# A product of zeros ahead of each wait for a landed chunk, in the first message pass of a graph kernel

## What is computed

```python
def rgcn_conv(x, src, dst, etype, W, root, bias):
    seg = dst * R + etype                      # R = 5 relations
    agg = segment_sum(x[src], seg)             # sum of neighbours by relation
    cnt = segment_sum(1, seg)
    agg = where(cnt > 0, agg / max(cnt, 1), 0).reshape(n, R, -1)
    return einsum('nrd,rdk->nk', agg, W) + x @ root + bias
h = relu(rgcn_conv(concat([x, node_emb[node_type]]), ...))     # 256 wide
```

## Time and profile before

| | us |
|---|---|
| median of 3 runs | 6255.49 (6251.28 to 6260.96) |
| the profiled execution, time | 6247.44 |
| its span | 6245.6 |
| TensorE busy | 4417.3 (71%) |
| GpSimd busy | 3267.3 (52%) |
| VectorE busy | 2981.6 (48%) |

### The profile page before, as it was taken

The page is one execution under the profiler, slowest core; times in us unless marked ns, Lnnn a source line. Parts: engine busy times, 40 slices in busy tenths (PEclk is TensorE's granted clock), DMA queues, the critical chain, the costliest instruction groups (busy, mean ns, idle before and its releaser), DMA issues.

```text
span 6245.6 us, 98864 instructions
## 1 busy us (share of the span) xinstructions
PE 4417.3 (71%) x20570; PEld 3106.2 (50%) x20573; DVE 2981.6 (48%) x6741; ACT 1057.7 (17%) x3779; POOL 3267.3 (52%) x3114
## 2 busy tenths in 40 slices
PE   4677676767677777777767777775647777877773
PEld 1223455555565445454544444444645665666652
DVE  5443222222222666667666666666882222222235
ACT  0111111111111111111111111111751111111112
POOL 0000355555554666666666666663325666666650
PEclk7566667777777999999999999997985555555556
DMA  1011223333333122222222222222423333333320
GB/s 67 23 53 53 79 85 93 102 92 102 95 104 106 53 61 72 71 81 81 90 74 61 65 71 77 82 79 74 147 94 85 85 85 85 84 84 85 84 73 11
DMA packets 318265, 492.02 MB, mean 79 GB/s; under 512 B 98090, under 2 KB 221228, under 8 KB 314556
## 3 DMA queue, kind: packets, MB, share of 16 engines
q0 software_dynamic: 108864, 246.74, 14.6%
q1 hardware_dynamic: 209372, 244.94, 11.8%
HBM read 406.11 MB, written 85.29 MB: 79 GB/s over the span
## 4 chain that ended last, share of the span: by engine, by line
issue 24%; POOL 22%; PE 19%; DMA 12%; DVE 9%; another core or an unknown queue 6%; DVEq 3%; ACTq 2%; ACT 2%; POOLq 1%; SPq 0%
POOL msg_r L493 22%; DMA msg_r<-y_tab,idx_r 8%; PE psum L1375 4%; DMA msg_r<-z_tab,idx_r 3%; PE psum L1440 3%; DVE h_t L1132 2%; PE psum L1255 1%; PE psum L1580 1%; DVE hot_r L990 1%; PE psum L1287 1%; PE psum L1267 1%; PE psum L1537 1%; ACT idx_r L578 1%; PE psum L1581 1%
## 5 line engine op out<-in xcount | busy, mean ns | idle before, releaser
L493 POOL DMA_INDIRECT msg_r<-y_tab,idx_r x2160 | 2234.6, 1035 | 2053.2 <-issue 1291.3
L1440 PE MATMUL psum<-shot_r,hotb_r 128*128 128x400 bf16 x5760 | 1313.6, 353 | 573.3 <-DMA msg_r<-y_tab,idx_r 454.8
L493 POOL DMA_INDIRECT msg_r<-z_tab,idx_r x882 | 933.6, 1058 | 511.5 <-issue 323.1
L1440 PEld LDWEIGHTS psum<-shot_r,hotb_r 128*128 128x128 bf16 x5760 | 503.4, 102 | 1009.4 <-DMA msg_r<-y_tab,idx_r 489.2
L1014 DVE TENSOR_SCALAR shot_r<-iota_h,edge_g 128x1600 bf16<-128x1600 f16 x1440 | 906.1, 684 | 0.0
L578 ACT COPY idx_r<-row_i 128x1 int32 x2142 | 409.9, 191 | 2898.6 <-DMA msg_r<-y_tab,idx_r 2643.2
L1580 PE MATMUL psum<-msg_r,shot_r 128*128 128x128 f32 x1764 | 680.2, 488 | 294.3 <-DMA msg_r<-z_tab,idx_r 152.1
L1375 PE MATMUL psum<-hot_r,msg_r 128*128 128x128 f32 x2880 | 634.5, 385 | 319.8 <-DVE hot_r L990 193.9
L1375 PEld LDWEIGHTS psum<-hot_r,msg_r 128*128 128x128 f32 x2880 | 540.9, 277 | 434.3 <-issue 260.9
L1580 PEld LDWEIGHTS psum<-msg_r,shot_r 128*128 128x128 f32 x1764 | 437.2, 308 | 522.8 <-DMA msg_r<-z_tab,idx_r 351.0
L893 DVE TENSOR_TENSOR shot_r<-iota_h,dst_g 128x384 f32<-128x384 f16 x294 | 166.1, 565 | 862.7 <-PE psum L1581 436.7
(11 more groups left out here) (273 smaller groups left out, 3905.3 us busy)
## 6 DMA issues: line engine op xcount, KB each, us to landing
msg_r<-in_attr SPq DMA_DIRECT2D x882, 64.0 KB
h_t<-count_tab SPq DMA_DIRECT2D x25, 1600.0 KB, 6.6
count_tab<-w_s SPq DMA_DIRECT2D x48, 800.0 KB
msg_r<-y_tab,idx_r POOLq DMA_INDIRECT x2160
xn<-heavy_tab SPq DMA_DIRECT2D x76, 320.0 KB
y_tab<-y_s SPq DMA_DIRECT2D x25, 640.0 KB, 2.9
xn<-y_tab SPq DMA_DIRECT2D x25, 640.0 KB
y_tab<-y_s SPq DMA_DIRECT2D x50, 320.0 KB
```

The source lines that it names most:

```text
L493: pool.indirect_dma_start(out=msg_r[:, q, 0:width], out_offset=None, in_=table, in_offset=bass.IndirectOffsetOnAxis(ap=idx_r[:, q:q + 1], ...
L1440: ins = T.matmul(psum[:, 4 + b, 0:CB], hotb_r[:, q, :], shot_r[:, q, b * CB:(b + 1) * CB], start=first, stop=last)
```

## The change

In the first pass TensorE executes one more product ahead of its wait for each chunk's rows: 128 columns of zeros times 512 columns of zeros in bf16, added to the whole bank of the open sums. So that the bank's other 256 columns take part in the open sums, the products that open and close a tile's sums are widened from 256 to 512 columns. What is computed stays the same. Nothing moves on the other engines.

```diff
                 for q in range(U):
                     if q % UH == 0:
                         pe.wait_ge(s_hot[k][q // UH], after)
+                    if k == 0:
+                        T.matmul(psum[:, bass.ds(slot, 1), :].rearrange("p o f -> p (o f)"), zeros_b[:, 0:P], zeros_b[:, :], start=False, stop=False)
                     pe.wait_ge(s_msg[k][q], landed)
...
             def start0(D, slot):
                 pe.wait_ge(s_inv_in, D)
-                clear(acc0(slot, 0, 2))
+                clear(psum[:, bass.ds(slot, 1), :].rearrange("p o f -> p (o f)"))
                 root0(D, lambda m: acc0(slot, m))
...
             def stop0(slot):
-                close(acc0(slot, 0, 2), s_sums[0])
+                close(psum[:, bass.ds(slot, 1), :].rearrange("p o f -> p (o f)"), s_sums[0])
```

## The result

The kernel after took 6277.85 us (median of 13 runs, 6257.29 to 6305.06) beside 6254.11 us for the kernel before (13 runs) on the same chip: a ratio of 1.0038, 95% interval 1.0026 to 1.0049, or 24 us slower. The forecast had the sign, and the time is inside the range, but 76 us were forecast, and 24 us lie outside the likeliest case's own +40 to +120 us. The two profiled executions differ by 17 us (6247.44 and 6264.57).

A forecast was written before the change was run, and what follows sets the result against it. No engine alone was taken to bound the kernel; in the first pass GpSimd's gathers wait for TensorE's chunks, at low clock 0.56 of the time. +91 - 17 + 2 = +76 us gave 6331 us, range 6230 to 6400 us.

The forecast's parts named there:

- likeliest case: Forecast case: low-clock share 0.35 to 0.8 in stretches behind one-hot waits, kernel +40 to +120 us; chance 0.58.
- The price of a product of zeros: A 512-column bf16 product of zeros on TensorE takes 0.22 us at the high clock, 0.44 us at the low.
- 267 zeros on the path, +91 us, less 17 us for the clock.: Three zeros in each of 89 groups with waiting one-hots delay chunks, +91 us; faster chunks give back 17 us.
- The low share of these stretches falls from 0.7 to 0.55: Low-clock share while three chunks run behind a wait for one-hots; the fall gains 17 us on chunks.
- the one-hots start 2.4 us behind the last gather whatever TensorE does: In groups with waiting one-hots, they follow the last gather's issue by 2.4 us, leaving TensorE that much to spare.
- groups that wait for their rows: I take 0: Zeros there run in 0.5 to 0.6 us of idle ahead of each chunk, so cost 0.
- the 2 us for all the other zeros: Each one-hot-waiting group's other three zeros and the widened opening and closing products are hidden ahead of line 1313: 2 us.
- The clock is high nearly everywhere: Rival: 267 zeros cost 59 us, chunks gain 81: -22 us, 6233 us; deciding low share 0.13; chance 0.12.
- The long waits are TensorE's own work at the low clock: Rival: high clock takes 1 us off about 100 VectorE waits, -100 us beside -22: 6135 us; chance 0.06.
- The zeros show everywhere: Rival: low share stays 0.7, other zeros of each tile's first two groups show: +154 us, 6410 us; chance 0.12.

The follow-up runs named there:

- g2: The changed kernel against the kernel before, on another chip of the slow kind: 1.0089, +54 us.
- f3: The changed kernel against the kernel before, on the fast chip: 0.9963, -21 us.
- e4: Kernel before plus widened opening and closing products and three 512-column zero products ahead of each wait for one-hots, none between chunks; slow-kind chip: 0.9969, -18 us.
- f2: Three zero products ahead of each wait for one-hots, none between chunks, against the kernel before on the fast chip: 0.9934, -37 us.
- e8: Eight zero products ahead of a tile's first group's one-hot wait and eight behind its heavy products, against the kernel before, fast chip: 1.0031, +18 us.
- e7: One zero product ahead of each wait for one-hots, two a group, against the kernel before on the fast chip: 0.9951, -28 us.
- e12: One zero product ahead of each wait for one-hots, two a group, against the kernel before on a slow-kind chip: 0.9982, -12 us.
- f4: One zero product directly ahead of each wait for one-hots, against the kernel before on the fast chip: 0.9955.
- f1: One zero product directly behind each wait for one-hots, against the kernel before on the fast chip: 0.9979.
- e11: Kernel before plus two semaphore additions ahead of each chunk's wait for rows, no zeros; slow-kind chip: 1.0039, +22 us.
- e5: Kernel before plus two semaphore additions ahead of each chunk's wait for rows, no zeros; fast chip: 1.0010.
- e10: The changed kernel against the kernel before, on a second slow-kind chip: 1.0082, +48 us.

## Why the prediction was right or wrong

**The price of a product of zeros** holds: 0.22 us high and 0.43 low between the starts of records, as medians of the traces after, g2 and f3 (1426.88 to 1427.10 and 1445.81 to 1446.24 above), where I had 0.22 and 0.44. Three chunks with their zeros take 2.0 us high and 3.8 low (I had 2.2 and 4.1).

**267 zeros on the path, +91 us, less 17 us for the clock.** This is 0.83 us for each of the 89 groups, and where the waits stay as they were it is right. In second groups the stretch from the first of the three chunks, or its zeros, to the end of the third grew by 1.07, 0.88 and 0.91 us on A, C and D, and the groups by 1.04, 0.84 and 0.82; in the first groups of C and D the stretch grew by 0.95 and 0.93. Line 1325 has 87 us of the chain on A and 98 on D (7.8% of 1260). In first groups of A the stretch grew by 0.28 us only, since the low share fell from 0.82 to 0.45. As time lost in the whole pass the term was too large: zeros ahead of the wait (e4, on B) are 42 us better than the change on A, 66 and 72 on C and D, and on F the place is worth 16 to 19 us (f2 against f3).

**"The low share of these stretches falls from 0.7 to 0.55"** holds in size: over all groups but the third it went from 0.73 to 0.58 on A, 0.81 to 0.62 on C and 0.78 to 0.64 on D. It doesn't hold in place. In the first two groups it stays at 0.75 on C and at 0.78 on D, and fell from 0.72 to 0.60 on A; the rest is in fourth and later groups. The chunk products lose 34 us of the chain on A, not 17. The clock of the pass rises more than I had (0.72 to 0.88, against 0.8), much of it in groups that wait for rows: the low share of third groups went to 0.00 and they became longer. The size of e4's gain, 18 us, agrees with the 17 only as a number.

**The step that failed** is that everything but the chunks stays where it is: **"the one-hots start 2.4 us behind the last gather whatever TensorE does",** and with it **"groups that wait for their rows: I take 0"** and the 2 us for all the other zeros. The rows shown for it are of a second group, and I carried it over to all 89. The runs show in its place:

- In first groups the one-hots came earlier after the change: 8.1 us behind the first gather where they had come 9.0 behind it on A (8.4 for 8.9 on C, 8.6 for 9.0 on D). That took 0.9 us off each on A and 0.5 on C and D; A's changed by -15 us where the forecast had +20.
- In third groups the zeros are hidden by the time of their records, as forecast, but TensorE's semaphore for the third chunk came late: +29 us where it had +7.
- In fourth groups the lateness of the third group's second half was gone: -33 us where it had +15. Before, their chunks waited 18 times for one-hots and once for rows, after 18 times for one-hots and 62 for rows.

By place in the tile, A's table is 57 us under the forecast: 35 in first groups and 48 in fourth, less 22 in third, 3 in second and 1 in later ones. That second groups came out at +23 where I had +20 is the part that was forecast for the right reason. C and D, at +48 and +54, have two thirds of the forecast; they too are under it most in fourth groups, by 16 and 21 us.

**The rivals.** "The clock is high nearly everywhere" is what happens on F: by the same reckoning the low share of all groups but the third is 0.05, below its 0.13, and the time is 21 us less where it had 22. The number is luck in part: F has neither the long idle times nor the late semaphores of the kind that I read, and its runs make the 21 us out of 37 gained by zeros in idle time (f2), less 16 to 19 for the place. "The long waits are TensorE's own work at the low clock" is half right on F, where the one-hots follow line 1313 at once (e8), though nothing gained more than 37 us; on the slow kind the waits end with late semaphores. "The zeros show everywhere" is out: no run comes near +154 us.

The Trainium skill, "TensorE: Matmul & The Clock Gate", section "Why this matters for your kernels", advised to keep TensorE busy. The traces agree on the clock (0.72 to 0.88). On the time they agree where the products stand ahead of the wait for one-hots in every group (e4, e7, e12, f2, f4), and on F behind it as well (f1, f3); behind it on A, C and D the same advice cost 0.4 to 0.9%.

**What stays open.** That instructions without a product cost time on the slow kind is shown by e11 (+22 us on C), and that they don't on F by e5. That they do it by moving the lateness rests on one trace each: the copy of the relations is 4.2 us late in e11's fourth groups, and 2.2 to 3.6 in the four traces without zeros. That the cause is the supply of instructions while gathers are in flight is argued, not shown; the traces speak against its nearest form, since from 920 to 2000 us no packet of the instruction queues (q8 and q14 on the page) moved in before, after, e10, e11 or g2, and the lateness is there throughout. What they do show is when it ends: where VectorE started late behind lines 1306 or 1313 (80 to 96 times a trace), it did so at most 2.8 us behind the start of the last gather, in all twelve traces of the slow kind. Why the change moves the lateness from one half of the third group to the other, why A's fourth groups gained and the others' hardly did, and what makes a chip one kind or the other stays open. So the cause of the forecast's miss is known by place and by wait, but not further.

## What to carry to other kernels

Products that only hold the clock up belong ahead of a wait that is idle anyway, and no more of them than lift the clock: three in idle time gained 0.3% on B and 0.7% on F, the same number behind the wait cost 0.4 to 0.9% on A, C and D and gained 0.4% on F, and a second one in each place cost 49 us at a clock that was full already. When an engine waits and the trace names no reason, or an unlikely one, compare the time from the producer's recorded end to the consumer's start over all places before calling it a rule of the program: the rule read in one group of a tile did not hold in the others. And time a change of a few tenths of a per cent on more than one chip: here its sign differed.

## What the runs showed of the hardware

- Two kinds of chip for one kernel: 6170 to 6260 us on four, 5630 us on one, 9 to 10% less, all at the same upper clock. In the first pass of the changed kernel the difference is 1.83 (A) against 1.49 us (F) a gather.
- On the slow kind VectorE's copy of the relations began up to 5.6 us behind the recorded end of the product it waits for while gathers were in flight (after; 4.2 us on the mean of e11's fourth groups); on the other 0.13 us on the mean in every place.
- In second groups of a tile the one-hots start 2.2 to 2.5 us behind the last gather's start, on the mean of each trace of the slow kind and whatever the program; on F between 0.7 us ahead of it and 0.6 behind, depending on the program.
- 1440 semaphore instructions added to TensorE, without a product, cost 22 us on C and at most 13 us (upper end of 1.0023) on F.
- The same kernel pair differed by +24, +48 and +54 us on three chips of one kind, with intervals 14 to 21 us wide.
